# A fused layer on one core: other steps for the sums and row copies of its attention, and 52 norm tiles on ScalarE

## Chip, core and metric

One core of a Trainium2 chip runs the whole program as one launch. The metric is the device time of one execution, in microseconds (us); lower is better. The core has five engines that take their instructions in order and wait for each other by counting semaphores: TensorE (PE), VectorE (DVE), ScalarE (ACT), GpSimd (POOL) and SyncE, which issues the DMAs.

## The reference

The input is 16 batches of 256 tokens of 128 numbers, float32. Four sublayers follow each other, each added to its input: a long convolution, a mixture of 8 experts (top 2), an attention, the same experts again. Each reads a layer norm of the stream. The change is in the attention:

```python
x = x + _L0_attn_b_ref(_layernorm(x, axis=-1), W_attn, W_proj)
# _L0_attn_b_ref: 16 heads of 8, four sets of queries, one set of keys and values
qkv = x @ W_attn.T
for g in range(4):
    att = softmax(where(causal, q_g @ k.T / sqrt(8), -inf))
    outs.append(att @ v)
return concatenate(outs, -1) @ W_proj.T
```

## The kernel before

**Stages.** Convolution, first experts, attention and second experts follow each other. While the attention runs, the last chunks of the first experts' result are normed for it, and its own results are normed for the second experts. A chunk is 4 tiles of 128 tokens, two batches.

**Time of the attention.** It runs in 256 steps, 16 in each batch: 4 quads of 4 heads, and 4 steps t = 0 to 3 in each quad. A step makes scores of heads against keys on TensorE (`tensor_scores`, line 1269) into one half of six PSUM banks, 1280 columns. Steps take the two halves in turn, so the scores of step n wait until the exp of step n-2 has read that half. ScalarE makes the exp of all 1280 columns in one instruction (`scalar_exp`, line 1296) into one of 8 buffers `prob`. GpSimd sets the masked entries to zero with affine selects, six in each quad (`gpsimd_mask`, line 1328).

**Blocks of tokens.** The 256 tokens of a batch are cut into four blocks of 64. The input holds the second half of the tokens in reverse. Blocks of queries against blocks of keys make three kinds of work: EARLY, ACROSS and LATE. EARLY and ACROSS have 512 columns a head (four query sets, two blocks), LATE 256. A quad's four steps hold each kind for each of its four heads (`STEPS_Q`, line 60).

**Sums.** `tensor_weigh` (line 1348) multiplies the values with the probabilities of one kind, 4 heads beside each other, as 8 instructions, adding ACROSS, EARLY and LATE up in bank 7. It is called for the quad before in steps 1, 2 and 3: `SUMS_Q = (ACROSS, EARLY, LATE)`. ACROSS waits until VectorE has turned the previous quad's sums out of bank 7. EARLY and LATE wait for masks. Value rows lie in `vstack`.

**VectorE's part.** `vector_turn` (line 1370) reads the finished sums with a stream transpose, inverts the denominators and scales, three instructions; `vector_rows` (line 1386) turns a batch's result for the projection, three transposes. `vector_attended` (line 1436) adds the projection to the stream. `vector_at_x_high` and `_low` copy the transposed tokens of batch b+2 out of PSUM in two float16 parts, `vector_qk_high` and `_low` the same for queries and keys, `vector_v` copies value rows. `vector_bounds` (line 1398) tests the inverted denominators once in four batches. Layer norms: statistics on VectorE (line 369), the power on GpSimd (line 383), and the tiles, (x - mean) * rstd, on VectorE (line 388), 4 in a chunk, two at step 9 and two at step 13.

**What is beside what.** No planner: the order of each engine is written out by step. In each step TensorE issues scores, then what `tensor_beside` (line 1834) holds for it, then the sum:

```python
if b + 2 < BATCH and at == 0:            tensor_at_x(e, b + 2)
if b + 2 < BATCH and at in (4, 8, 12):   tensor_qk(e, b + 2, at // 4 - 1)
if 0 < b < BATCH - 1 and at in (7, 11):  tensor_project(e, b - 1, at // 8)
if b + 1 < BATCH and at == 15:           tensor_v(e, b + 1)
```

Token transposes (line 1124), q/k products (1168), projections (1432) and value rows (1235) all use bank 6, so each waits until VectorE has copied the one before out of it: transposes wait for `v_copied`, q/k products of steps 8 and 12 for `attn_done` (the projection of the batch before is added), projections for `lo_done` and for `rows_up`. VectorE's order beside is in `vector_beside` (line 1871): rows at step 5, residuals at 6 and 10, value copies at 14, the turn ahead of all else at step 3 of a quad. In the first 16 steps nothing is projected. SyncE writes and reads back q/k parts through DRAM for the batches ahead; the change leaves that as it is.

After the last step, `tensor_second` (line 1722) sums the last quad between the first products of the second experts.

Of the kernel before, what the change touches and what calls it, by code (L numbers as in the profile page):

```python
# [13 lines left out]
ALU = mybir.AluOpType  # L14
# [3 lines left out]
P = 128  # L18
# [46 lines left out]
SUMS_Q = (ACROSS, EARLY, LATE)  # L65
STEPS_B = 4 * QUADS
SUMS_B = len(SUMS_Q) * QUADS
# [77 lines left out]
def build_in(nc, dr, out, ctx):  # L145
# [150 lines left out]
    def new_norm(tag):  # L296
# [21 lines left out]
        "conv_mean_negated", "offset_ready", "mean_negated", "route_offset", "conv_normed_by_scalar", "first_folded", "fold_sums", "fold_differences"))  # L318

# [445 lines left out]

    def tensor_xt(e, m, ch):
# [345 lines left out]
    def tensor_at_x(e, b):  # L1112
# [10 lines left out]
        for at, h in ((0, 1), (P, 1), (P + BLK, 0)):  # L1123
            last = e.transpose(bank(at_bank(b))[:, at:at + P], normed[:, HALVES * b + h, :], eye[:])
        last.then_inc(at_up, 1)
# [3 lines left out]

# [92 lines left out]
    def tensor_v(e, b):  # L1222
# [7 lines left out]
        for kind in (EARLY, LATE, ACROSS):  # L1230
            for i, (w_part, x_part) in enumerate(PRODUCTS):
                for half in range(HALVES if kind != ACROSS else 1):
                    rows = slice(BLK * half, BLK * (half + 1)) if kind != ACROSS else slice(0, P)
                    token = P * half + BLK * kind if kind != ACROSS else P
# [34 lines left out]
    def tensor_scores(e, n):  # L1269
# [12 lines left out]
        for kind, lane, col in STEPS_Q[t]:  # L1282
            at = slice(SLOT * lane, SLOT * (lane + 1))
            queries = qstack[at, s, c].rearrange("p g (h l q) -> p h l g q", h=HALVES, q=BLK)
            for half in range(HALVES):
                rows = slice(BLK * half, BLK * (half + 1))
                if kind == EARLY:
                    key, moving, place = P * half, queries[:, half], to[rows, col:col + BANK]
                elif kind == LATE:
                    key, moving, place = P * half + BLK, queries[:, half, 1], to[rows, col:col + SETS * BLK]  # L1290
                else:
                    key, moving, place = P + BLK * half, queries[:, 0], to[rows, col:col + BANK]
# [3 lines left out]
    def scalar_exp(e, n):  # L1296
        if n >= PROBS:
            e.wait_ge(weighed, len(SUMS_Q) * ((n - PROBS) // 4 + 1))
# [29 lines left out]
    def gpsimd_mask(e, n):  # L1328
# [3 lines left out]
        if t == 0:  # L1332
            gpsimd_second_half_mask(e, m)
            if q:
                gpsimd_first_half_mask(e, m - 1)
# [4 lines left out]
        elif t == 3:  # L1340
            gpsimd_second_half_mask(e, m + 2)

# [27 lines left out]
    def vector_turn(e, t):  # L1370
        b, c, _ = step_of(4 * t)
        r = t % 2
        e.wait_ge(weighed, len(SUMS_Q) * (t + 1))
# [12 lines left out]
    def vector_rows(e, b):  # L1386
        e.wait_ge(o_normed, QUADS * (b + 1))
        if b:
            e.wait_ge(projected, HALVES * b)

        blocks = o_norm[:, 0].rearrange("p (g l n) r -> p g l (n r)", g=SETS, l=2)
        rows = o_rows[:, 0].rearrange("p g (l t) -> p g l t", l=2)
        for late in range(2):
            e.transpose(rows[:, :, 1 - late], blocks[:, :, late])  # L1394
        e.transpose(o_rows[:, 1].rearrange("p g t -> p (g t)"), o_norm[:, 1].rearrange("p n r -> p (n r)"))\
         .then_inc(rows_up, 1)
# [19 lines left out]
    def tensor_project(e, b, h):  # L1416
        e.wait_ge(rows_up, b + 1)
# [822 lines left out]
```

## Time and profile before

| what | value |
|---|---|
| three runs | 790.78, 791.18, 791.28 us; median 791.18 |
| the profiled execution | 789.12 us, its span 787.4 us |
| busy share of the span | PE 93%, ACT 86%, DVE 84%, POOL 71% |
| attention, first exp to last | starts at 245.1 and 592.8 us of the span |
| granted TensorE clock | 0.999 of full speed over the span |

Busy time is a union of instruction durations; ends of matmuls are modelled, so distances between starts are the firmer reading. "idle ... <- X" is the time an engine stood still just before instructions and what released it. PE is the multiplying part of TensorE, PEld its weight loads. Line numbers are those of the kernel before.

### The profile page before, as it was taken

Reading aid. Unit: us, or ns where it says so; the run is one execution under the profiler, and the core shown is the slowest. Engines: PE = TensorE matmul, PEld = TensorE weight load, DVE = VectorE, ACT = ScalarE, POOL = GpSimd, SP = SyncE. Lnnn points to the kernel's source line nnn. Section 1 sums busy time; section 2 is a strip of 40 time slices with the busy share of each in tenths; the row PEclk is TensorE's granted clock in tenths of the full one; section 3 lists DMA queues with packets and bytes.
Section 4 is the critical chain, followed back from the end, with each engine's and each line's share of the span. In section 5 each row is a group of like instructions: output and inputs, shape, how many; then the busy total and the mean of one; then the engine's idle time right before and its main releaser. Section 6 shows DMA issues by size and latency. Waiting matters only on the chain.

```text
span 787.4 us, 21234 instructions
## 1 busy us (share of the span) xinstructions
PE 736.1 (93%) x8090; PEld 404.9 (51%) x8090; DVE 660.6 (84%) x1955; ACT 677.5 (86%) x934; POOL 562.6 (71%) x623
## 2 busy tenths in 40 slices
PE   5798999999999999999999999999888999999996
PEld 3345667777775233333333333333334777677774
DVE  7998999899876867879788888788487889989885
ACT  5918999999999988888898898888987999899984
POOL 2898676655446989999999999989995445445542
PEclk9999999999999999999999999999999999999999
DMA  9210000000044244533543333453400000000000
GB/s 271 64 80 28 2 2 2 2 2 2 2 109 109 73 95 97 101 87 89 108 108 100 96 97 98 92 96 82 99 2 1 10 7 14 15 15 15 15 14 18
DMA packets 37964, 45.74 MB, mean 58 GB/s; under 512 B 6137, under 2 KB 23810, under 8 KB 37858
## 3 DMA queue, kind: packets, MB, share of 16 engines
q1 hardware_dynamic: 37858, 44.33, 23.0%
q8 instruction: 66, 1.08, 0.6%
q14 instruction: 40, 0.33, 0.2%
HBM read 27.53 MB, written 16.78 MB: 56 GB/s over the span
## 4 chain that ended last, share of the span: by engine, by line
PE 61%; DVE 24%; issue 6%; ACT 5%; POOL 4%; DMA 0%; DVEq 0%; ACTq 0%; POOLq 0%
PE psum L1015 15%; PE psum L1365 14%; PE psum L946 14%; PE psum L1432 4%; PE psum L1293 4%; DVE mixed L1034 4%; PE psum L1168 3%; DVE o_tok L1375 2%; DVE vstack L1261 2%; PE psum L1235 2%; ACT hidden_first L960 1%; ACT hidden_parts_first L962 1%; PE psum L695 1%; DVE parts L1193 1%; DVE o_rows L1394 1%
## 5 line engine op out<-in xcount | busy, mean ns | idle before, releaser
L1300 ACT ACTIVATE prob<-psum 128x1280 f32<-128x1280 f32 x256 | 304.6, 1240 | 43.0 <-PE psum L1293 36.3
L1309 POOL TENSOR_SCALAR_AFFINE_SELECT prob<-prob 128x768 f32<-128x768 f32 (+1 forms) x384 | 308.1, 840 | 27.0 <-ACT prob L1300 26.9
L946 PE MATMUL psum<-xt_parts,w_parts 128*128 128x512 f16 x768 | 186.6, 379 | 0.0
L1365 PE MATMUL psum<-prob,vstack 128*32 128x512 f32 (+1 forms) x1536 | 177.3, 533 | 6.4 <-DVE o_tok L1375 4.4
L976 POOL TENSOR_TENSOR hidden_parts_second<-hidden_second,hidden_parts_second 128x512 f16<-128x512 f32 x64 | 77.7, 1213 | 94.8 <-ACT hidden_parts_second L962 94.8
L1034 DVE SCALAR_TENSOR_TENSOR mixed<-psum,comb_y,mixed 128x128 f32<-128x128 f32 x512 | 143.1, 339 | 1.6 <-PE psum L1015 1.5
L976 POOL TENSOR_TENSOR hidden_parts_first<-hidden_first,hidden_parts_first 128x512 f16<-128x512 f32 x64 | 79.2, 1238 | 73.0 <-ACT hidden_parts_first L962 73.0
L1293 PE MATMUL psum<-qstack,kstack 32*64 32x512 f16 (+1 forms) x1536 | 103.4, 362 | 1.9 <-ACT prob L1300 1.8
L1293 PEld LDWEIGHTS psum<-qstack,kstack 32*64 32x64 f16 x1536 | 29.9, 101 | 145.9 <-ACT prob L1300 125.2
L946 PEld LDWEIGHTS psum<-xt_parts,w_parts 128*128 128x128 f16 x768 | 70.9, 98 | 64.9 <-issue 1.4
L960 ACT ACTIVATE hidden_second<-psum,b 128x512 f32<-128x512 f32 x128 | 88.3, 690 | 17.3 <-PE psum L946 12.3
L1015 PEld LDWEIGHTS psum<-w_parts,hidden_parts_first 128*128 128x128 f16 x1536 | 90.3, 98 | 19.6 <-issue 6.7
L1015 PE MATMUL psum<-w_parts,hidden_parts_first 128*128 128x128 f16 x1536 | 96.2, 219 | 3.9 <-DVE mixed L1034 3.4
L1015 PEld LDWEIGHTS psum<-w_parts,hidden_parts_second 128*128 128x128 f16 x1536 | 90.8, 98 | 16.5 <-issue 2.5
L1015 PE MATMUL psum<-w_parts,hidden_parts_second 128*128 128x128 f16 x1536 | 96.0, 219 | 1.0 <-POOL hidden_parts_second L976 0.5
L960 ACT ACTIVATE hidden_first<-psum,b 128x512 f32<-128x512 f32 x128 | 90.3, 705 | 7.2 <-PE psum L946 6.4
L962 ACT ACTIVATE hidden_parts_first<-psum,b 128x512 f16<-128x512 f32 x128 | 90.5, 707 | 0.0
L962 ACT ACTIVATE hidden_parts_second<-psum,b 128x512 f16<-128x512 f32 x128 | 88.4, 691 | 0.0
L969 DVE TENSOR_TENSOR hidden_parts_second<-hidden_second,hidden_parts_second 128x512 f16<-128x512 f32 x64 | 57.3, 896 | 17.8 <-ACT hidden_parts_second L962 17.8
L1375 DVE STREAM_TRANSPOSE o_tok<-psum 128x512 f32<-128x512 f32 x64 | 45.7, 713 | 25.4 <-PE psum L1365 25.4
L969 DVE TENSOR_TENSOR hidden_parts_first<-hidden_first,hidden_parts_first 128x512 f16<-128x512 f32 x64 | 49.6, 776 | 16.9 <-ACT hidden_parts_first L962 16.9
L1365 PEld LDWEIGHTS psum<-prob,vstack 128*32 128x32 f32 x1536 | 30.2, 108 | 45.4 <-issue 28.0
(150 smaller groups left out, 859.6 us busy)
## 6 DMA issues: line engine op xcount, KB each, us to landing
qstack<-qk_parts SPq DMA_DIRECT2D x128, 128.0 KB, 3.6
qk_parts<-parts SPq DMA_DIRECT2D x64, 192.0 KB, 3.2
kstack<-qk_parts SPq DMA_DIRECT2D x128, 32.0 KB, 3.5
stream<-u_folded SPq DMA_DIRECT2D x4, 512.0 KB, 8.2
kept_x<-stream SPq DMA_DIRECT2D x4, 512.0 KB, 2.7
out<-mixed SPq DMA_DIRECT2D x7, 256.0 KB, 2.3
w_whole<-L_ffn_W SPq DMA_DIRECT2D x1, 1024.0 KB, 9.6
taps<-c_taps SPq DMA_DIRECT2D x1, 640.0 KB, 7.7
```

The source lines that it names most:

```text
L946: last = e.matmul(bank(u % 4), m.w1[:, w_part, ex, cols], xt_parts[:, s, x_part, :], start=(n == 0), stop=(n == len(PRODUCTS) - 1))
L960: last = e.activation(m.hidden[:, r, k, :], bank(u % 4), ACT.Relu, scale=scale, bias=bias)
L962: last = e.activation(m.hidden_parts[:, r, 0, k, :], bank(u % 4), ACT.Relu, scale=scale, bias=bias)
L969: e.tensor_tensor(m.hidden_parts[:, r, 1, 0, :], m.hidden[:, r, 0, :], m.hidden_parts[:, r, 0, 0, :], ALU.subtract).then_inc(low_first, 1)
L976: e.tensor_tensor(m.hidden_parts[:, r, 1, 1, :], m.hidden[:, r, 1, :], m.hidden_parts[:, r, 0, 1, :], ALU.subtract).then_inc(low_second, 1)
L1015: last = e.matmul(down_place(m, ch, ex, t), h_[:, t * P:(t + 1) * P], w_, start=(n == 0), stop=(n == len(terms) - 1))
L1034: last = e.scalar_tensor_tensor(out=m.y[:, t0 + t, :], in0=down_place(m, ch, ex, t), scalar=comb_y[:, s, t, ex:ex + 1], in1=m.y[:, t0 + t, ...
L1293: last = e.matmul(place, kstack[at, s, c, key:key + BLK], moving, start=True, stop=True)
L1300: e.activation(prob[:, n % PROBS, 0:COLS], psum[:, TILE * (n % 2):TILE * (n % 2) + COLS], ACT.Exp, scale=SCALE)\
L1309: return e.affine_select(kept, kept, [[0, n] for n in kept.shape[1:-1]] + [[sign, BLK]], ALU.is_ge, 0.0, base=BLK * half, channel_multipli ...
L1365: last = e.matmul(to[SLOT * lane:SLOT * (lane + 1)], vstack[:, b % 2, kind, c * LANES + lane].rearrange("p h r -> p (h r)"), weights_of(q, ...
L1375: e.transpose(o_tok[:, r, :].rearrange("p (g l t) -> p g l t", l=2, t=BLK), by_token).then_inc(turned, 1)
```

## The change

- EARLY and LATE sums of the quad before stand together in step 2, ACROSS alone in step 1, nothing in step 3 (`SUMS_Q`). The turn moves from step 3 to step 2.
- Blocks get other kinds, so that EARLY and LATE use 128 rows of one token stretch: 12 products for value rows in place of 15. The three token transposes write the blocks to other places.
- Token transposes move from step 0 to step 2, their copies on VectorE too, ahead of the turn. Rows move from step 5 to 3, residuals from 6 and 10 to 7 and 11, value copies from 14 to 15. Rows are released in two parts, each to its projection.
- The second mask of a LATE pair moves to step 3, from the next quad's step 0.
- 13 chunks' norm tiles move to ScalarE: x * rstd + offset with Identity, behind the exps of steps 9 and 13; VectorE makes offset = -mean * rstd for 4 tiles in one instruction at step 6.

```diff
@@ -62,9 +62,11 @@
 COLS = 2 * BANK + SETS * BLK
-SUMS_Q = (ACROSS, EARLY, LATE)
+SUMS_Q = ((), (ACROSS,), (EARLY, LATE), ())
+KINDS = 3
 STEPS_B = 4 * QUADS
-SUMS_B = len(SUMS_Q) * QUADS
+SUMS_B = KINDS * QUADS
 MASKS_Q = 3
@@ -316,6 +318,7 @@
         "conv_mean_negated", "offset_ready", "mean_negated", "route_offset", "conv_normed_by_scalar", "first_folded", "fold_sums", "fold_differences"))
+    beside_offset = sem("offset_beside_attention")
@@ -762,6 +765,50 @@
+    @dataclass
+    class Beside:
+        norm: object
+        i: int
+        x: object
+        ch: int
+        n: int
+    def chunk_normed(b):
+        if b % 2 == 0 and b // 2 + 2 < FFN_CHUNKS:
+            return mixed_norm, b // 2 + 2
+        return (expert_norm, (b - 3) // 2) if b % 2 and b >= 3 else None
+    def normed_beside(b):
+        held = chunk_normed(b)
+        if held is None:
+            return None
+        norm, ch = held
+        n = sum(chunk_normed(before) is not None for before in range(b))
+        return Beside(norm, ch, mixed, ch, n) if norm is mixed_norm else Beside(norm, second.at + ch, stream, ch, n)
+    def vector_offset_beside(e, of):
+        tiles = slice(of.ch * FFN_TILES, (of.ch + 1) * FFN_TILES)
+        e.wait_ge(of.norm.rstd, of.i + 1)
+        e.scalar_tensor_tensor(out=offset[:, tiles], in0=meanvar[:, tiles, 0], scalar=-1.0, in1=rstd[:, tiles],
+                               op0=ALU.mult, op1=ALU.mult).then_inc(beside_offset, 1)
+    def scalar_normed_beside(e, of, half):
+        if half == 0:
+            e.wait_ge(beside_offset, of.n + 1)
+            if of.norm is mixed_norm:
+                e.wait_ge(xt_up, of.ch + 1)
+            else:
+                e.wait_ge(at_up, FFN_TILES // HALVES * (of.ch + 1))
+        t0 = of.ch * FFN_TILES + half * FFN_TILES // 2
+        for t in range(t0, t0 + FFN_TILES // 2):
+            last = e.activation(normed[:, t, :], of.x[:, t, :], ACT.Identity, scale=rstd[:, t:t + 1],
+                                bias=offset[:, t:t + 1])
+        if half:
+            last.then_inc(of.norm.out, 1)
@@ -1120,13 +1167,14 @@
-        for at, h in ((0, 1), (P, 1), (P + BLK, 0)):
-            last = e.transpose(bank(at_bank(b))[:, at:at + P], normed[:, HALVES * b + h, :], eye[:])
-        last.then_inc(at_up, 1)
+        to = bank(at_bank(b))
+        for at in (0, P + BLK):
+            e.transpose(to[:, at:at + P], normed[:, HALVES * b + 1, :], eye[:])
+        e.transpose(to[:, P:3 * P].rearrange("p (l h t) -> p l h t", h=HALVES, t=BLK)[:, :, 0], normed[:, HALVES * b, :],
+                    eye[:]).then_inc(at_up, 1)
@@ -1229,9 +1277,9 @@
             for i, (w_part, x_part) in enumerate(PRODUCTS):
-                for half in range(HALVES if kind != ACROSS else 1):
-                    rows = slice(BLK * half, BLK * (half + 1)) if kind != ACROSS else slice(0, P)
-                    token = P * half + BLK * kind if kind != ACROSS else P
+                for late in range(2 if kind == ACROSS else 1):
+                    rows = slice(BLK * late, BLK * (late + 1)) if kind == ACROSS else slice(0, P)
+                    token = P * late + BLK if kind == ACROSS else P * kind
                     last = e.matmul(bank(6)[rows, kind * P:(kind + 1) * P],
@@ -1281,21 +1329,21 @@
             at = slice(SLOT * lane, SLOT * (lane + 1))
-            queries = qstack[at, s, c].rearrange("p g (h l q) -> p h l g q", h=HALVES, q=BLK)
+            queries = qstack[at, s, c].rearrange("p g (l h q) -> p h l g q", h=HALVES, q=BLK)
             for half in range(HALVES):
...
                 if kind == EARLY:
-                    key, moving, place = P * half, queries[:, half], to[rows, col:col + BANK]
+                    key, moving, place = BLK * half, queries[:, half], to[rows, col:col + BANK]
                 elif kind == LATE:
-                    key, moving, place = P * half + BLK, queries[:, half, 1], to[rows, col:col + SETS * BLK]
+                    key, moving, place = P + BLK * half, queries[:, half, 1], to[rows, col:col + SETS * BLK]
                 else:
-                    key, moving, place = P + BLK * half, queries[:, 0], to[rows, col:col + BANK]
+                    key, moving, place = P * half + BLK, queries[:, 0], to[rows, col:col + BANK]
                 last = e.matmul(place, kstack[at, s, c, key:key + BLK], moving, start=True, stop=True)
...
         if n >= PROBS:
-            e.wait_ge(weighed, len(SUMS_Q) * ((n - PROBS) // 4 + 1))
+            e.wait_ge(weighed, KINDS * ((n - PROBS) // 4 + 1))
         e.wait_ge(scored, n + 1)
@@ -1331,14 +1379,13 @@
             gpsimd_second_half_mask(e, m)
-            if q:
-                gpsimd_first_half_mask(e, m - 1)
         elif t == 1:
...
             gpsimd_second_half_mask(e, m + 2)
+            gpsimd_first_half_mask(e, m + 2)
@@ -1370,7 +1417,7 @@
         r = t % 2
-        e.wait_ge(weighed, len(SUMS_Q) * (t + 1))
+        e.wait_ge(weighed, KINDS * (t + 1))
         by_token = bank(7).rearrange("p (l g t) -> p g l t", l=2, t=BLK)
@@ -1387,13 +1434,14 @@
             e.wait_ge(projected, HALVES * b)
+        e.transpose(o_rows[:, 1].rearrange("p g t -> p (g t)"), o_norm[:, 1].rearrange("p n r -> p (n r)"))\
+         .then_inc(rows_up, 1)
...
         for late in range(2):
-            e.transpose(rows[:, :, 1 - late], blocks[:, :, late])
-        e.transpose(o_rows[:, 1].rearrange("p g t -> p (g t)"), o_norm[:, 1].rearrange("p n r -> p (n r)"))\
-         .then_inc(rows_up, 1)
+            last = e.transpose(rows[:, :, 1 - late], blocks[:, :, late])
+        last.then_inc(rows_up, 1)
@@ -1414,7 +1462,7 @@
     def tensor_project(e, b, h):
-        e.wait_ge(rows_up, b + 1)
+        e.wait_ge(rows_up, HALVES * b + h + 1)
         if b + 3 < BATCH:
@@ -1832,7 +1880,7 @@
     def tensor_beside(e, b, at):
-        if b + 2 < BATCH and at == 0:
+        if b + 2 < BATCH and at == 2:
             tensor_at_x(e, b + 2)
@@ -1854,8 +1902,9 @@
             tensor_beside(e, *STARTS[n])
-            if n >= 4 and n % 4:
-                tensor_weigh(e, n // 4 - 1, SUMS_Q[n % 4 - 1])
+            if n >= 4:
+                for kind in SUMS_Q[n % 4]:
+                    tensor_weigh(e, n // 4 - 1, kind)
@@ -1863,38 +1912,36 @@
             scalar_exp(e, n)
+            b, at = STARTS[n]
+            if at in (9, 13) and normed_beside(b):
+                scalar_normed_beside(e, normed_beside(b), at // 12)
             if n == LAST - STEPS_B:
...
     def vector_beside(e, b, at):
-        if b + 2 < BATCH and at == 0:
-            vector_at_x_high(e, b + 2)
-            vector_at_x_low(e, b + 2)
         if b + 2 < BATCH and at in (4, 8, 12):
...
             vector_qk_low(e, b + 2, at // 4 - 1)
-        if b and at == 5:
+        if b and at == 3:
             vector_rows(e, b - 1)
...
             vector_bounds(e, b // BOUNDED - 1, at // 4)
-        if b and at in (6 if b + 1 < BATCH else 9, 10):
-            vector_attended(e, b - 1, at // 10)
-        if b + 1 < BATCH and at == 14:
+        if b and at in (7 if b + 1 < BATCH else 9, 11):
+            vector_attended(e, b - 1, at // 11)
+        if b + 1 < BATCH and at == 15:
...
                 vector_mixed_stats(e, b // 2 + 2)
-            elif at in (9, 13):
-                vector_mixed_normed_half(e, b // 2 + 2, at // 12)
         if b % 2 and b >= 3:
...
                 vector_route_stats(e, second, (b - 3) // 2)
-            elif at in (9, 13):
-                vector_second_normed_half(e, (b - 3) // 2, at // 12)
+        if at == 6 and normed_beside(b):
+            vector_offset_beside(e, normed_beside(b))
         if b == 12 and at % 2:
@@ -1909,9 +1956,13 @@
         for n in range(LAST):
-            if n % 4 == 3 and n >= 4:
+            b, at = STARTS[n]
+            if at == 2 and b + 2 < BATCH:
+                vector_at_x_high(e, b + 2)
+                vector_at_x_low(e, b + 2)
+            if n % 4 == 2 and n >= 4:
                 vector_turn(e, n // 4 - 1)
-            vector_beside(e, *STARTS[n])
+            vector_beside(e, b, at)
@@ -1923,7 +1974,6 @@
             gpsimd_mask(e, n)
-        gpsimd_first_half_mask(e, MASKS_Q * QUADS * BATCH - 1)
```

## Rows read from the trace of the kernel before

**Rows 1.** page, section 4: the chain that ended last, by engine

```profile
PE 61%; DVE 24%; issue 6%; ACT 5%; POOL 4%; DMA 0%; DVEq 0%; ACTq 0%; POOLq 0%
```

**Rows 2.** page, section 5: the exps and the masks

```profile
L1300 ACT ACTIVATE prob<-psum 128x1280 f32<-128x1280 f32 x256 | 304.6, 1240 | 43.0 <-PE psum L1293 36.3
L1309 POOL TENSOR_SCALAR_AFFINE_SELECT prob<-prob 128x768 f32<-128x768 f32 (+1 forms) x384 | 308.1, 840 | 27.0 <-ACT prob L1300 26.9
```

**Rows 3.** batch 6: us, then busy us of PE, PEld, DVE, ACT, POOL, clock, DMA

```profile
375.77:397.49 21.72, 21.10 (x241) 7.77 (x241) 17.45 (x42) 19.09 (x16) 19.96 (x26) 1.00 0.45 98
```

**Rows 4.** timeline of batch 6, PE: start us, us, engine, line, op, names, count

```profile
376.87 1.07 PE L1365 MATMUL psum<-prob,vstack 128*32 128x512 f32 x8
377.87 0.41 PE L1293 MATMUL psum<-qstack,kstack 32*64 32x512 f16 x6
...
379.54 0.64 PE L1365 MATMUL psum<-prob,vstack 128*32 128x256 f32 x8
380.11 0.41 PE L1293 MATMUL psum<-qstack,kstack 32*64 32x512 f16 x6
380.45 0.83 PE L1168 MATMUL psum<-at_x,wqkv_parts 128*128 128x256 f16 x6
381.21 0.41 PE L1293 MATMUL psum<-qstack,kstack 32*64 32x512 f16 x6
...
383.87 0.41 PE L1293 MATMUL psum<-qstack,kstack 32*64 32x512 f16 x6
384.46 1.16 PE L1432 MATMUL psum<-wproj,o_rows 128*128 128x128 f32 x8 [0.18 <-DVE o_rows L1395]
385.55 0.64 PE L1365 MATMUL psum<-prob,vstack 128*32 128x256 f32 x8
...
395.66 0.80 PE L1235 MATMUL psum<-wqkv_parts,at_x 128*64 128x128 f16 x15
396.39 0.64 PE L1365 MATMUL psum<-prob,vstack 128*32 128x256 f32 x8
396.96 0.41 PE L1293 MATMUL psum<-qstack,kstack 32*64 32x512 f16 x6
397.80 0.52 PE L1124 MATMUL psum<-eye,normed 128*128 128x128 f32 x3 [0.44 <-DVE vstack L1261]
```

**Rows 5.** timeline of batch 6, ACT: the first exp of batch 7

```profile
397.49 1.24 ACT L1300 ACTIVATE prob<-psum 128x1280 f32<-128x1280 f32 x1 [0.40 <-PE psum L1293]
```

**Rows 6.** timeline of batch 0, where PE waited for an exp

```profile
248.78 3.50 ACT L1300 ACTIVATE prob<-psum 128x1280 f32<-128x1280 f32 x3 [0.61 <-PE psum L1293]
...
250.07 0.41 PE L1293 MATMUL psum<-qstack,kstack 32*64 32x512 f16 x6 [0.60 <-ACT prob L1300]
```

**Rows 7.** waits between 270 and 620 us: in total, times, longest

```profile
PE psum L1124 <- DVE vstack L1261: 5.3, 12, 0.4
PE psum L1432 <- DVE o_rows L1395: 5.0, 13, 1.3
```

**Rows 8.** timeline of batch 6, DVE: a turn, the next copy, a residual

```profile
380.24 0.72 DVE L1375 STREAM_TRANSPOSE o_tok<-psum 128x512 f32<-128x512 f32 x1 [0.57 <-PE psum L1365]
...
381.73 0.68 DVE L1193 TENSOR_SCALAR parts<-psum 128x512 f16<-128x512 f32 x1
...
385.65 0.29 DVE L1442 TENSOR_TENSOR stream<-psum,mixed 128x128 f32<-128x128 f32 x1 [1.25 <-PE psum L1432]
```

**Rows 9.** groups by line, 270 to 620 us: the upper bound test

```profile
L1407 DVE SCALAR_TENSOR_TENSOR in_bounds<-rden,in_bounds 128x512 f32<-128x512 f32 x3 | 3.2, 1065 | 0.0
```

**Rows 10.** timeline of the first expert layer, ACT: four norm tiles

```profile
64.00 1.67 ACT L747 ACTIVATE normed<-stream,offset,rstd 128x128 f32<-128x128 f32 x4
65.53 0.70 ACT L960 ACTIVATE hidden_first<-psum,b 128x512 f32<-128x512 f32 x1
```

**Rows 11.** timeline at the end of the attention, PE

```profile
592.14 0.41 PE L1293 MATMUL psum<-qstack,kstack 32*64 32x512 f16 x6
...
595.62 1.06 PE L1365 MATMUL psum<-prob,vstack 128*32 128x512 f32 x8 [2.50 <-DVE o_tok L1375]
```

## The prediction

> **What bounds the kernel now.** I read the chain of waits first. TensorE holds 61% of the chain that ended last, VectorE 24% and ScalarE 5% [rows 1]. The change touches the attention, the stretch of 256 exps; there ScalarE sat idle 43.0 us before exps, 36.3 of them for score products on TensorE [rows 2]. So I asked for one batch of the attention by itself, batch 6 counted from 0: 21.72 us long, with TensorE busy 21.10 us, GpSimd 19.96, ScalarE 19.09 and VectorE 17.45 [rows 3]. The reader should see that TensorE has no room, and ScalarE 2.63 us.
>
> TensorE's timeline of that batch gives the price of each piece, taken from its start to the start of the next one, for the ends are modelled [rows 4]. One step's scores take 0.335 us (0.34 from 380.11 to 380.45, 0.33 in others), a sum over ACROSS or EARLY 1.00 (376.87 to 377.87), over LATE 0.57 (379.54 to 380.11), a q/k product 0.76, a projection half 1.09, the value rows 0.73. Two places are longer than that: from the scores at 383.87 to the projection 0.59, hence 0.255 of waiting for rows, and from the scores at 396.96 to the token transposes 0.84, hence 0.505 of waiting for VectorE's value copies. Work is then 21.72 - 0.255 - 0.505 = 20.96 us.
>
> Two more distances decide this case. An exp begins 0.53 to 0.54 us after its scores begin, when ScalarE is idle (396.96 [rows 4] to 397.49 [rows 5]), and lasts 1.24. Scores begin 0.05 us after the exp that frees their half of PSUM: the exp that began at 248.78 ended at 250.02, and TensorE, idle 0.60 us, began at 250.07 [rows 6]. PSUM holds two steps. So from the start of step n's scores to the start of step n+2's scores there lie **at least 0.54 + 1.24 + 0.05 = 1.83 us**, whatever TensorE has to do.
>
> **Why the old order rarely meets that floor.** The sums lie at steps 1, 2 and 3 of each quad, ACROSS, EARLY, LATE. Around the light steps 3 and 0, step 3's LATE and whatever lies beside fill the time: 0.335 + 0.57 + 0.335 + 0.76 = 2.00, more than 1.83. In rows 6 there are no sums yet at steps 2 and 3, and there TensorE waits; that is the case the new order makes everywhere.
>
> **The change, part by part.**
>
> *Sums.* EARLY and LATE both come at step 2, none at step 3. The number of products stays. Step 2 becomes 1.57 us of sums after its scores, so step 3's scores come late, ScalarE idles before its exp, and that exp begins 0.54 us after them. Then the floor of 1.83 runs from step 3.
> - Step 15 to step 1 of the next batch: TensorE has 0.335 + value rows + 0.335. The value rows go from 15 products to 12, EARLY and LATE on 128 rows at once: 0.73 x 12/15 = 0.58. That is 1.25 of work against 1.83: a **wait of 0.58**, where the token transposes (moved to step 2) used to stand.
> - Step 3 to step 5: 0.335 + 0.335 + 0.76 = 1.43 against 1.83: **0.40**.
> - Steps 7 and 11 carry a projection, 1.09, so the floor is met there: nothing.
>
> *Residual behind the projection.* The q/k product of step 8 waits until VectorE has read the projection of step 7 out of the same bank. LATE used to stand between the two; now only the scores of step 8 do. Count from the end of LATE at step 6. TensorE: 0.335 + 1.09 + 0.335 = 1.76. VectorE: it starts the turn 0.13 us after LATE's slot ended (380.11 [rows 4], 380.24 [rows 8]), and is free again 1.49 us later (381.73); then comes the new offset operation, 4 columns, about 0.25 by my estimate from such short ones, bounds 0.15 and 0.6; then the residual, 0.29 and some 0.07 to the release. Together 0.13 + 1.49 + 0.25 + 0.36 = 2.23, a **wait of 0.47**, or 0.22 in batches without a norm. Step 12 has no offset: **0.22**. In batches 5, 9 and 13 the upper bound test, 1.07 us [rows 9], stands in that same chain at step 6 and adds its length.
>
> *Waits taken away.* The token transposes at step 2 no longer stand behind the value copies, and the rows are turned at step 3, long before step 7. The two waits were 5.3 and 5.0 us over 12 and 13 batches in the stretch from 270 to 620 us [rows 7]. By start distances I count 0.505 and 0.255.
>
> *Norms.* 52 tiles leave VectorE, 4 in each of 13 batches; ScalarE makes them, behind the exps of steps 9 and 13. ScalarE had four in a row from 64.00 to the next instruction at 65.53, 0.385 each [rows 10]: 0.77 at each place, 1.54 in a batch, 20.0 in all. It had 2.63 us idle [rows 3]. The norms push the exp of steps 10 and 14 back by up to 0.77, but the exp behind it waits for the scores of steps 11 and 15, which stand behind the double sum and come about that much late themselves. So I take **0**, with only 0.1 us to spare; uncovered they cost up to 20.0. VectorE is not the bound, so its relief is also worth 0, except at the end.
>
> *Sum for batch 6.* Work 20.96 - 0.15 = 20.81; waits 0.58 + 0.40 + 0.47 + 0.22 = 1.67; 22.48 against 21.72: +0.76.
>
> *Sum for the stage.* New waits: 14 x 0.58 = 8.1; 13 x 0.40 = 5.2 (batch 0 has it already); 11 x 0.47 + 2 x 0.22 + 3 x 1.07 = 8.8; 13 x 0.22 = 2.9; together 25.0. Gone: 14 x 0.505 = 7.1; the waits for rows 5.0, with 13 x 0.08 for start distances 6.0; value rows 15 x 0.15 = 2.3; together 15.4. Net +9.6.
>
> *The end.* After the last scores at 592.14 TensorE's next sum came at 595.62, with 2.50 us idle for VectorE, whose turn stood behind two norm tiles [rows 11]. Now that turn comes one step earlier and the tiles are gone; the sum needs only the last exp, 1.83 + 0.02 after the scores: 3.48 - 1.85 = -1.6 us. Against it, in batch 15 the first transposes still wait for value copies, and with no LATE in between for 0.57 more; I add 0.6 for that and 0.5 for masks and startup, where GpSimd is closest to its limit. Total **+9.1**. The profiled execution took 789.1, which gives 798.2; the median of the runs is 791.2, 2.1 above it, so I forecast **800.3**.
>
> **A rule against this reading.** TensorE's 21.10 of 21.72 us is my reason to call it the bound; its timeline shows distances that repeat to 0.01 us. The Trainium skill (Perfetto Trace Analysis, Identifying the Most-Contended Engine) says that matmul busy time does not show how near TensorE is to its limit, and that occupancy does for the others. By it GpSimd or ScalarE would be asked first, and what ScalarE is given would count in full: the second rival below.
>
> **Rivals.**
> 1. *TensorE waits for nothing.* If scores don't meet the floor, because the pairs of sums run closer together than two separate ones and ScalarE catches up, only the removed waits count: 15.4 + 1.6 = 17.0 less, 774; with half of the new waits 787. It decides from where the new waits sum to less than 15.9 instead of 25.0. For it: TensorE is the bound and its waits fall. Against it: rows 6 show the wait where no sum stands, and the floor holds two rows' distances only. Chance 0.12. If LATE right behind EARLY saves 0.1 us, 64 times, that is 794, still in my forecast.
> 2. *ScalarE becomes the bound.* If an activation from SBUF between two exps costs more than 0.385, or the exp behind it can't overlap it, the 0.1 us to spare is gone at 26 places: 20.0 more at the very most, about 820; with a quarter of it 805. Against: 2.63 us idle. Chance 0.08.
> 3. *Nothing to speak of.* The two orders give each other back what they take: the pieces are the same, and GpSimd, 19.96 of 21.72, sets the pace after all, as 384 masks of 0.84 [rows 2] don't change. Then 789.6 to 792.8. Against: the last mask of a quad is ready about 1.3 us before LATE needs it, by two short masks behind the exp of step 3 against 0.05 + 0.335 + 1.00 + 0.335 + 1.00. Chance 0.06.
>
> **The numbers.** Forecast 0.74, its own range 793 to 807. Under 788 lies most of rival 1, over 807 a part of rival 2; so 788 to 807. A measurement of this kernel tells 0.2%, 1.6 us. Faster 0.13, same 0.06, slower 0.81.
>
> **What would show it.** In a middle batch: length 22.4 to 22.5; TensorE idle for ScalarE before the scores of steps 1 and 5, 0.6 and 0.4; before the q/k products of steps 8 and 12 for VectorE, 0.5 and 0.2, and over 1 at step 8 in batches 5 and 9; ScalarE idle about 0.6 or more before each exp of a step 3; no wait before the transposes and projections; about 1.5 us between last exp and the next work less than before. A middle batch under 21.7 or ScalarE without idle time would prove me wrong.

## The result, and the profile after

The changed kernel took 814.34 us (median of 4 runs, 813.36 to 819.12), against 791.23 for the kernel before beside it: ratio 1.0304, 95% interval 1.0263 to 1.0345. It is 23.1 us slower. The forecast had the side right (slower, 0.81) and the size wrong: 800.3, range 788 to 807.

The page of the kernel after, sections 1, 2 (the clock alone) and 5 (the exps, as in [rows 2]):

```profile
span 812.2 us, 21151 instructions
...
PE 735.3 (91%) x8042; PEld 411.7 (51%) x8042; DVE 638.8 (79%) x1916; ACT 692.8 (85%) x986; POOL 565.3 (70%) x623
...
PEclk9999999999999999998999999999999999999999
...
L1348 ACT ACTIVATE prob<-psum 128x1280 f32<-128x1280 f32 x256 | 302.4, 1241 | 52.8 <-PE psum L1341 52.4
```

Every engine's share fell, TensorE's busy time is what it was (735.3 us against 736.1), and the span grew by 24.8 us. So time was lost in waits, of all engines at once. The attention, from the first exp to the end of the last, grew from 348.9 to 374.9 us (it ran from 245.1 to 620.0); what follows it shrank by 1.1.

TensorE's waits, 270 to 620 us, as in [rows 7] (in total, times, longest):

```profile
PE psum L1216 <- DVE stream L1490: 22.7, 26, 2.5
...
PE psum L1341 <- ACT prob L1348: 14.9, 30, 1.3
```

Both old waits, for value copies and for rows, are gone, as foreseen; only the first transposes of the second experts, in batch 15, still wait for value copies, 1.9 us. L1216, the q/k product, waits 22.7 us for the residual L1490, L1341, the scores, 14.9 us for exps. Batch 6 of the kernel after, TensorE, from the first scores behind the exps of steps 15 and 3 to the product of step 8, as in [rows 4]:

```profile
385.63 0.41 PE L1341 MATMUL psum<-qstack,kstack 32*64 32x512 f16 x6
385.97 0.80 PE L1283 MATMUL psum<-wqkv_parts,at_x 128*128 128x128 f16 x12
386.70 0.41 PE L1341 MATMUL psum<-qstack,kstack 32*64 32x512 f16 x6
387.46 0.41 PE L1341 MATMUL psum<-qstack,kstack 32*64 32x512 f16 x6 [0.35 <-ACT prob L1348]
...
391.04 0.52 PE L1341 MATMUL psum<-qstack,kstack 32*64 32x512 f16 x12
391.50 0.83 PE L1216 MATMUL psum<-at_x,wqkv_parts 128*128 128x256 f16 x6
392.87 0.41 PE L1341 MATMUL psum<-qstack,kstack 32*64 32x512 f16 x6 [0.54 <-ACT prob L1348]
...
394.54 1.50 PE L1412 MATMUL psum<-prob,vstack 128*32 128x512 f32 x16
395.97 0.41 PE L1341 MATMUL psum<-qstack,kstack 32*64 32x512 f16 x6
396.30 1.16 PE L1480 MATMUL psum<-wproj,o_rows 128*128 128x128 f32 x8
397.39 0.41 PE L1341 MATMUL psum<-qstack,kstack 32*64 32x512 f16 x6
399.26 0.81 PE L1216 MATMUL psum<-at_x,wqkv_parts 128*128 128x256 f16 x6 [1.46 <-DVE stream L1490]
```

Two readings. From the scores of step 15 at 385.63 to those of step 1 at 387.46 lie 1.83 us, and from step 3 at 391.04 to step 5 at 392.87 again 1.83: the floor of the forecast, to the hundredth. But the product of step 8 waited 1.46, not 0.47. What VectorE did meanwhile, as in [rows 8]:

```profile
396.10 0.72 DVE L1422 STREAM_TRANSPOSE o_tok<-psum 128x512 f32<-128x512 f32 x1 [0.60 <-PE psum L1412]
396.86 0.35 DVE L1425 RECIPROCAL rden<-o_tok 128x32 f32<-128x32 f32 x1
397.25 1.15 DVE L1427 TENSOR_TENSOR o_norm<-o_tok,rden 128x256 f32<-128x256 f32 x1
398.31 0.60 DVE L796 SCALAR_TENSOR_TENSOR offset<-meanvar,rstd 128x4 f32<-128x4 f32 x1
398.84 0.28 DVE L1490 TENSOR_TENSOR stream<-psum,mixed 128x128 f32<-128x128 f32 x1
```

The order is the one forecast; the scaling of the turn took 1.15 us where the turn's 1.49 [rows 8] has it at 0.42, and four columns of offset took 0.60. In that time GpSimd's masks ran without a pause:

```profile
395.50 5.00 POOL L1357 TENSOR_SCALAR_AFFINE_SELECT prob<-prob 128x768 f32<-128x768 f32 x6
```

The clock is the second thing. Stretches of the kernel after (us, busy us of PE, PEld, DVE, ACT, POOL, granted clock, DMA share, GB/s); [rows 3] has 1.00 for batch 6 of the kernel before:

```profile
369.00:381.00 12.00, 9.48 (x81) 3.67 (x74) 6.42 (x11) 6.62 (x8) 7.67 (x9) 0.72 0.32 65
387.30:410.40 23.10, 20.47 (x238) 8.12 (x238) 16.30 (x40) 20.27 (x22) 20.29 (x25) 1.00 0.37 93
410.30:435.00 24.70, 22.06 (x238) 8.24 (x238) 16.30 (x40) 20.41 (x22) 20.29 (x25) 0.93 0.36 86
```

In batch 5 (first line) the bound test stands in the chain too, the product of step 8 waited 2.52 us, and with that wait TensorE's granted clock fell from 2.4 to 1.2 GHz for 6.8 us:

```profile
373.62 1.44 PE L1216 MATMUL psum<-at_x,wqkv_parts 128*128 128x256 f16 x6 [2.52 <-DVE stream L1490]
374.99 0.64 PE L1341 MATMUL psum<-qstack,kstack 32*64 32x512 f16 x6
375.56 1.94 PE L1412 MATMUL psum<-prob,vstack 128*32 128x512 f32 x8
377.42 0.64 PE L1341 MATMUL psum<-qstack,kstack 32*64 32x512 f16 x6
```

A q/k product took 1.37 us from start to start instead of 0.76, an ACROSS sum 1.86 instead of 1.00. The same happened in batches 0, 7, 9 and 15 for 3.4 us each. That has its price in the lengths: a middle batch took 23.05 us, but batch 7, with the same waits, 24.64, batch 5 26.70 and batch 9 25.62.

### The profile page after: what moved, and what is told of

Its sections match the earlier page's. It is cut to its first block and busy times, and to the rows that moved or that the text cites. A ratio compares the mean times of both kernels' runs of the same rounds, so it can differ in the third digit from the quotient of the medians.

```text
span 812.2 us, 21151 instructions
## 1 busy us (share of the span) xinstructions
PE 735.3 (91%) x8042; PEld 411.7 (51%) x8042; DVE 638.8 (79%) x1916; ACT 692.8 (85%) x986; POOL 565.3 (70%) x623
## 3 DMA queue, kind: packets, MB, share of 16 engines
q8 instruction: 66, 1.08, 0.6%
## 5 line engine op out<-in xcount | busy, mean ns | idle before, releaser
L1412 PE MATMUL psum<-prob,vstack 128*32 128x512 f32 (+1 forms) x1536 | 170.2, 546 | 1.9 <-ACT prob L1348 1.9
L1341 PE MATMUL psum<-qstack,kstack 32*64 32x512 f16 (+1 forms) x1536 | 101.5, 368 | 17.6 <-ACT prob L1348 17.6
L1007 ACT ACTIVATE hidden_second<-psum,b 128x512 f32<-128x512 f32 x128 | 88.3, 690 | 15.9 <-PE psum L993 12.3
L1341 PEld LDWEIGHTS psum<-qstack,kstack 32*64 32x64 f16 x1536 | 28.9, 102 | 122.7 <-ACT prob L1348 84.5
L1412 PEld LDWEIGHTS psum<-prob,vstack 128*32 128x32 f32 x1536 | 37.2, 110 | 71.0 <-issue 64.9
```

The source lines that it names most:

```text
L1007: last = e.activation(m.hidden[:, r, k, :], bank(u % 4), ACT.Relu, scale=scale, bias=bias)
L1341: last = e.matmul(place, kstack[at, s, c, key:key + BLK], moving, start=True, stop=True)
L1412: last = e.matmul(to[SLOT * lane:SLOT * (lane + 1)], vstack[:, b % 2, kind, c * LANES + lane].rearrange("p h r -> p (h r)"), weights_of(q, ...
```

## Experiments

Medians of the kernel before beside them were 790.7 to 790.9 us. A middle batch is one like batch 6.

### Norms back on VectorE, norms alone on ScalarE

```diff
 # norms_on_vector, against the changed kernel: 52 tiles by
-                scalar_normed_beside(e, normed_beside(b), at // 12)
-            vector_offset_beside(e, normed_beside(b))
+                vector_mixed_normed_half(e, b // 2 + 2, at // 12)
+                vector_second_normed_half(e, (b - 3) // 2, at // 12)
 # scalar_norms_old_order, against the kernel before: the same the other way round
```

> The changed kernel with its 52 norm tiles back on VectorE (mean and rstd, at steps 9 and 13), the offset operation gone. Theory 1 (TensorE waits behind VectorE's chain turn, offset, residual at step 8, and behind the exps of steps 3 and 15): only the offset's 0.6 us leaves that chain, so a middle batch falls from 23.05 to about 22.4 us, some of the half-clock stretches go, and the time is 800 to 809. Theory 2 (the norms on ScalarE are what costs): all of the loss goes, 789 to 795.

> The kernel before with the 52 norm tiles alone moved to ScalarE (scale and offset, behind the exps of steps 9 and 13), all sums, rows, transposes and residuals at their old steps. Theory 1: ScalarE's idle time covers them, and the residual stands ahead of the offset operation: 788 to 795, a middle batch 21.7 to 22.0. Theory 2: most of the loss shows here too, 805 to 815.

With the norms back: 801.98 us, ratio 1.0166 (1.0130 to 1.0202); a middle batch 22.52. With the norms alone moved: 789.67 us, ratio 0.9993 (0.9982 to 1.0004); middle batches 21.72, as before, with the waits of [rows 7] unchanged (5.3 and 4.9 us). Theory 1 holds in both, theory 2 in neither. In the new order, too, ScalarE's tiles don't hold TensorE: with them back on VectorE it still waited 0.35 and 0.54 us for exps in a middle batch, as in the changed kernel. ScalarE's 52 tiles cost nothing in the old order (28 and 24 of them):

```profile
L804 ACT ACTIVATE normed<-stream,offset,rstd 128x128 f32<-128x128 f32 x28 | 12.2, 490 | 0.0
L804 ACT ACTIVATE normed<-mixed,offset,rstd 128x128 f32<-128x128 f32 x24 | 10.5, 493 | 0.0
```

In the new order what costs is the offset on VectorE, 0.53 us in a middle batch (23.05 - 22.52; the wait at step 8 fell from 1.46 to 0.94), about 6 us over 11 batches with a projection and a norm; the rest of those 12.4 us are clock stretches that are gone (in this run two of 3.4 us stand in the attention, where there were 20.4 us).

### The q/k product one step later

```diff
-        if b + 2 < BATCH and at in (4, 8, 12):
+        if b + 2 < BATCH and at in (4, 9, 13):
```

> The changed kernel with the q/k products of steps 8 and 12 (and VectorE's copies of them) at steps 9 and 13, so that TensorE has scores and more between a projection and the product that waits for its residual. Theory 1: the wait of 1.46 and 0.22 us in a batch goes, nearly all of it, the floor behind the exps stays: a middle batch 21.4 to 22.2 us, no half-clock stretch, 788 to 799. If the waits behind the exps were the larger part instead, the batch stays above 22.5 and the time above 803.

A miss: 807.85 us, ratio 1.0233 (1.0209 to 1.0258), a middle batch 22.69. By the bound in the expectation the larger part would go to the waits for exps. The trace says why it doesn't: in a middle batch the product still waited 1.05 us for the residual. Step 8 has no sum in the new order, so going from step 8 to step 9 passes only one set of scores, 0.335 us. The expectation had counted a step as a step of the old order. The next run takes the wait away by another edit.

### The residual ahead of the turn

```diff
 # on VectorE, batches 1 to 14: at steps 6 and 10 no turn;
 # at steps 7 and 11, after vector_beside has issued the residual:
+            if behind:
+                vector_turn(e, n // 4 - 1)
```

> The changed kernel with one thing different on VectorE: in batches 1 to 14 the turn that belongs to steps 6 and 10 comes behind the residual of steps 7 and 11, so that the residual no longer stands behind the turn, only behind the offset operation. Theory 1 (the chain turn, offset, residual holds the q/k product of step 8): the wait of 1.46 us falls to 0.1 to 0.3, that of 0.22 to about 0.1, a middle batch is 21.4 to 21.9 us, the half-clock stretches behind those waits go, and the time is 788 to 796. If the chain is not what holds it, or the turn is then late for the next ACROSS sum, the batch stays over 22.5 and the time over 803.

793.49 us, ratio 1.0034 (1.0019 to 1.0049): of 23 us lost, 20 are back with one reordering on VectorE. A middle batch is 21.72, the q/k products wait 0.27 us in it, and the scores still 0.97 for exps. TensorE and clock in the same two stretches as above:

```profile
369.00:381.00 12.00, 11.43 (x140) 4.21 (x139) 8.27 (x19) 11.63 (x14) 10.91 (x15) 1.00 0.44 96
387.30:410.40 23.10, 21.85 (x258) 8.69 (x251) 15.96 (x40) 21.28 (x22) 21.78 (x28) 1.00 0.38 93
```

After batch 0 the clock no longer fell in the attention of this profiled execution (791.27 us, mean clock 0.992). That isn't so of every execution: seven of the ten had a mean clock of 0.986 to 0.988 and took 793.3 to 794.9 us, so some stretches stay; where they lie, no trace shows. What remains of the loss is less than batch 0 alone, 25.36 us instead of 20.81, in which the products of step 4 waited 1.25 us for the token copies and the clock fell for 6.8 us.

### Small masks

```diff
-            return prob[:, slot].rearrange("p (n l g q) -> p n l g q", n=3, l=2, q=BLK)[:, :, 0]
-        return prob[:, slot:slot + 2, 2 * BANK:COLS].rearrange("p n (g q) -> p n g q", q=BLK)
+            return prob[:, slot].rearrange("p (n l g q) -> p n l g q", n=3, l=2, q=BLK)[:, 0:1, 0]
+        return prob[:, slot:slot + 1, 2 * BANK:COLS].rearrange("p n (g q) -> p n g q", q=BLK)
```

> The changed kernel with each mask cut to a third or a half of its columns (256 in place of 768 and 512), so most masked entries stay in the sums: a part of the masking is left out. Theory 1a (VectorE's operations with two SBUF inputs wait for a mask in progress on GpSimd, which makes the scaling of the turn 1.15 us long at step 6 and the offset 0.6): the scaling at step 6 falls towards 0.42 to 0.6, the offset towards 0.1 to 0.3, the wait before the q/k product of step 8 from 1.46 to 0.4 to 0.8, a middle batch to 22.0 to 22.4. Theory 1b (the scaling is long for another reason): nothing changes there.

This kernel leaves out most of the masking. 792.79 us (one execution), a middle batch 21.87, a little under its range; TensorE waited 0.50 us for residuals in it instead of 1.68. Of the 1.18 us that the batch lost, 1.17 are the wait at step 8 (0.29 for 1.46), while the waits for exps stayed 0.35 and 0.54. VectorE's two operations, 280 to 580 us, first with small masks, then in the changed kernel:

```profile
L1427 DVE TENSOR_TENSOR o_norm<-o_tok,rden 128x256 f32<-128x256 f32 x54 | 22.9, 425 | 1.9
L796 DVE SCALAR_TENSOR_TENSOR offset<-meanvar,rstd 128x4 f32<-128x4 f32 x11 | 2.3, 211 | 0.0
```

```profile
L1427 DVE TENSOR_TENSOR o_norm<-o_tok,rden 128x256 f32<-128x256 f32 x51 | 29.8, 585 | 1.8
L796 DVE SCALAR_TENSOR_TENSOR offset<-meanvar,rstd 128x4 f32<-128x4 f32 x11 | 6.6, 602 | 0.0
```

Scaling 425 ns against 585, offset 211 against 602: theory 1a. Nothing in those operations changed, only how long GpSimd's instructions beside them are. The trace of the changed kernel says it of each operation. Of the 63 scalings in the attention 44 took 0.50 us or less; the other 19 took 0.78 to 1.16, and each of them ended 0.27 us after a mask did. The 11 offsets of 0.60 us all ended within 0.01 us after a mask; the two that met no mask in progress took 0.15.

The Trainium skill (SBUF — State Buffer, SBUF: two separate sides) says that a VectorE operation with two SBUF inputs and a GpSimd operation that reads SBUF contend for a shared port pair, and that whichever starts first holds it for its whole instruction. The trace agrees for the masks: the scaling, two SBUF inputs, took 1.15 us beside long ones and 0.425 on average beside short ones, and its late ends follow theirs. It isn't seen with every GpSimd instruction: the scaling in the turn of [rows 8], 0.42 us at 381.38, ran beside GpSimd's power of 4 columns, recorded from 381.33 for 1.00 us (spans on GpSimd are rough). The forecast had no term for any of this.

### The sums alone

```diff
-SUMS_Q = (ACROSS, EARLY, LATE)
+SUMS_Q = ((), (ACROSS,), (EARLY, LATE), ())
 # turn at n % 4 == 2, second LATE mask at step 3; nothing else of the change
```

> The kernel before with the sums and what goes with them alone moved: EARLY and LATE at step 2, the turn at step 2, the second mask of a LATE pair at step 3; the old blocks, norms on VectorE, transposes at step 0, rows at 5, residuals at 6 and 10, value copies at 14 stay. Theory 1: this alone brings most of the loss: waits behind the exps of step 3 (0.4 to 0.55) and, at step 0, for value copies with nothing beside them (0.5 becomes about 1.1), and the residual behind the turn, 0.5 to 1.2 at step 8; a middle batch 22.5 to 23.6, the time 803 to 820. Theory 3 (the loss needs the moved transposes and residuals too): 790 to 799.

827.17 us, ratio 1.0462 (1.0440 to 1.0485), above the range that I gave: the sums alone cost 36 us, so the rest of the change gives 13 back. Where they cost (270 to 620 us):

```profile
PE psum L1125 <- DVE vstack L1262: 17.6, 12, 1.5
PE psum L1169 <- DVE stream L1442: 13.2, 26, 1.9
PE psum L1294 <- ACT prob L1301: 9.5, 16, 1.1
```

The token transposes at step 0 wait 1.47 us for value copies each time, 17.6 us in all, where it was 5.3 before [rows 7]; in the changed kernel, with the transposes at step 2, this wait is gone. Batches without a bound test took 23.02 us at full clock and 24.7 to 24.8 with a half-clock stretch; ten such stretches stand in the attention after batch 0.

### LATE back at step 3

```diff
-SUMS_Q = ((), (ACROSS,), (EARLY, LATE), ())
+SUMS_Q = ((), (ACROSS,), (EARLY,), (LATE,))
 # turn at step 3, rows at 5, residuals at 6 and 10, value copies at 14;
 # the second run, in batch 0 alone: transposes and copies at step 0
-        if b + 2 < BATCH and at == 2:
+        if b + 2 < BATCH and at == (2 if b else 0):
```

> The changed kernel with LATE sums back at step 3, the turn with them, residuals at 6 and 10, rows at 5, value copies at 14; the new blocks, the norms on ScalarE, the transposes at step 2 and the rows in two parts stay. Theory 1: both kinds of waits go, since LATE stands again between scores of steps 3 and 0 and between projection and q/k product: TensorE without waits, a middle batch 20.9 to 21.6, 780 to 790. Theory 2: ScalarE's norms stay, so 805 to 815.

> The kernel with LATE back at step 3, and in batch 0 alone the token transposes and their copies at step 0 as in the kernel before, ahead of the statistics on VectorE. In the run without this TensorE waited 1.25 us at step 4 of batch 0 and the clock then stood at half for 3.4 us. Theory 1: that wait and that stretch go, batch 0 falls from 23.6 to 21.0 to 22.3 us, the time to 785 to 787.5. If the clock falls all the same, 787.5 to 789.

788.05 us, ratio 0.9969 (0.9954 to 0.9985), and with the repair of batch 0 786.05 us, ratio 0.9945 (0.9928 to 0.9962): both beat the changed kernel by over 26 us, the second one the kernel before by 4.7. Batch 0 fell from 23.61 to 20.83 us, 2.78 less: its wait of 1.25 and, so, 1.53 for a stretch of 3.4 us at half clock (its range was 21.0 to 22.3). No wait for residuals is left in a middle batch; its length, 21.70, missed its range of 20.9 to 21.6 by 0.1, since one wait for an exp is left (batch 7 of the second run):

```profile
394.33 0.41 PE L1341 MATMUL psum<-qstack,kstack 32*64 32x512 f16 x6
394.67 0.80 PE L1283 MATMUL psum<-wqkv_parts,at_x 128*128 128x128 f16 x12
395.40 0.64 PE L1412 MATMUL psum<-prob,vstack 128*32 128x256 f32 x8
395.96 0.41 PE L1341 MATMUL psum<-qstack,kstack 32*64 32x512 f16 x6
396.85 0.41 PE L1341 MATMUL psum<-qstack,kstack 32*64 32x512 f16 x6 [0.48 <-ACT prob L1348]
```

Steps 15 and 0 hold 0.34 + 0.73 + 0.56 + 0.34 = 1.97 us, more than the floor, yet the scores of step 1 wait. Here the exp of step 15 began 1.23 us after its scores, since the two norm tiles behind the exp of step 13 had pushed the exps of steps 14 and 15. Taking the old wait of 0.505 away had opened another of 0.48. So a middle batch is as long as before (21.70 against 21.72); the gain over the kernel before stands in batches whose waits were longer than in a middle one (batches 1 and 12, 0.8 and 0.9 us shorter) and behind the attention (191.9 us against 193.3). Three more runs asked whether the wait can be closed.

### What still holds the middle batch

```diff
 # norms_at_7_and_11, against the last kernel
-            if at in (9, 13) and normed_beside(b):
+            if at in (7, 11) and normed_beside(b):
-        if at == 6 and normed_beside(b):
+        if at == 5 and normed_beside(b):
 # turn_ahead_of_values: that, and value copies at step 15, behind the turn
-        if b + 1 < BATCH and at == 14:
+        if b + 1 < BATCH and at == 15:
```

> The kernel with LATE back at step 3 and the repaired batch 0, with ScalarE's norm tiles behind the exps of steps 7 and 11 in place of 9 and 13, and the offset at step 5. In the run without this ScalarE sat idle 0.76 and 0.38 us before the exps of steps 8 and 12, and none before that of step 15, whose lateness (0.48 us before the scores of step 1) I put down to the norms of step 13. If so: that wait goes, a middle batch is 21.1 to 21.4, the time 779 to 783. If the wait of 0.48 has another source, the batch stays at 21.7 and the time at 785 to 787.

> The same kernel with LATE at step 3 and the repaired batch 0, with the norm tiles back on VectorE at steps 9 and 13. If the norms on ScalarE cause the 0.48 us: a middle batch 21.2 to 21.5, the time 780 to 785, with some loss at the end of the attention, where the last turn stands behind two norm tiles again (about 1.5 us). If they don't: 785 to 789.

> The kernel with LATE at step 3, the repaired batch 0 and ScalarE's norms at steps 7 and 11, with one thing more: VectorE's value copies at step 15, behind the turn in place of ahead of it. In the run without this the ACROSS sum of step 1 waited 0.79 us for that turn, which stood behind 1.16 us of value copies. If that is the last hold of the middle batch: the wait falls to 0.2 to 0.4, the token transposes of step 2 may wait up to 0.4 for the value copies, a middle batch is 21.0 to 21.5, the time 777 to 784. If a third constraint keeps 21.70, the time stays at 785 to 787.

All three missed their favoured ranges, and the last two lay above both of theirs. Norms at 7 and 11: 786.09 us, ratio 0.9944 (0.9931 to 0.9956), the middle batch still 21.70. The cause of the 0.48 was right, no exp is waited for there any more; but the turn behind the value copies took its place at once:

```profile
397.56 1.06 PE L1412 MATMUL psum<-prob,vstack 128*32 128x512 f32 x8 [0.79 <-DVE o_tok L1422]
```

Norms on VectorE with LATE at step 3: 790.97 us, ratio 1.0006 (0.9995 to 1.0018), middle batches 21.96, with 0.88 us of that same wait. In this order ScalarE's norms are thus worth 5 us (790.97 against 786.05). The turn ahead of the value copies: 797.1 us, ratio 1.0085 (1.0072 to 1.0099). The wait for the turn fell to 0.31 as expected, but the value copies came so late that the transposes waited 1.03:

```profile
400.87 0.85 DVE L1427 TENSOR_TENSOR o_norm<-o_tok,rden 128x256 f32<-128x256 f32 x1
401.64 1.15 DVE L1309 TENSOR_SCALAR vstack<-psum 64x256 f32<-64x256 f32 x3
...
404.25 0.41 DVE L1186 CAST at_x<-psum 128x256 f16<-128x256 f32 x1
```

The scaling took 0.85 us where a mask ran beside it. So between the sums of step 15 and those of step 2 VectorE has a turn and the value copies, about 2.7 us, and whichever comes second is waited for. 786.05 us is the best that these runs reached.

## Why the prediction was right or wrong

**Right: what bounds, the floor, the waits that go.** TensorE's time is work plus waits; the distance of 1.83 us came out to the hundredth, at both places; both old waits went. ScalarE's norms cost TensorE nothing in the old order and in the new one, as two runs show: 22.7 us more work for ScalarE, and 789.67 us; rival 2 falls, and so does the reading by occupancy that stood behind it. The end of the attention gained 1.2 us against 1.6 (from the last scores to the next sum 2.26 us instead of 3.48).

**Sizes in the middle batch, forecast and measured:**

| term, by start distances | forecast | measured |
|---|---|---|
| scores of step 1, for the exp of 15 | 0.58 | 0.43 |
| scores of step 5, for the exp of 3 | 0.40 | 0.61 |
| q/k product of step 8, for the residual | 0.47 | 1.54 |
| q/k product of step 12 | 0.22 | 0.29 |
| a double sum, four in a batch | 1.57 | 1.43 |
| value rows, 12 products | 0.58 | 0.73 |
| scores of steps 3 and 4 together | 0.67 | 0.46 |
| batch | 22.48 | 23.05 |

The two floor terms together are 0.98 against 1.04. The step that failed is the third: "0.13 + 1.49 + 0.25 + 0.36 = 2.23, a **wait of 0.47**". It took the turn's length from one place [rows 8] as if it were fixed, and the offset from short operations. Both depend on what GpSimd does at that moment. The rest of the chain was right: with small masks the term came to 0.37, and the forecast's own chain gives 0.38 with the 0.16 that the offset took there in place of 0.25. The trace of the kernel before already held the price, ten scalings of 0.66 to 0.95 us in its attention. Its turn at 386.25 met only the last 0.23 us of a mask; its scaling took 0.50 us, and the next masks began after it:

```profile
387.39 0.50 DVE L1380 TENSOR_TENSOR o_norm<-o_tok,rden 128x256 f32<-128x256 f32 x1
```

```profile
387.96 4.71 POOL L1309 TENSOR_SCALAR_AFFINE_SELECT prob<-prob 128x768 f32<-128x768 f32 x6 [0.33 <-ACT prob L1300]
```

In the new order the turn before step 8 falls into a row of six masks. Scaling 0.73 more (1.15 for 0.42) and offset 0.35 more (0.60 for 0.25) make 1.08, and the term came out 1.07 larger; over 11 batches that is 11.8 us. The value rows failed too: I scaled 0.73 by 12/15, but 12 products took as long as 15. The traces say why. Products of 64 rows start in pairs, less than 0.01 us apart, and from one pair to the next it is mostly 0.05 to 0.06 us, as between two products of 128 rows. The kernel before had 6 pairs and 3 products of 128 rows, the changed one has 3 pairs and 6 products: 9 places in both.

**Wrong by omission: the clock and batch 0.** No term of the sum held the possibility that the clock falls behind longer waits. In the profiled execution six drops, five of them in the attention, came to 20.4 us at half speed there. Batches 5, 7 and 9 were 2.6, 1.6 and 1.5 us longer than waits explain (26.70 - 23.05 - 1.06; 24.64 - 23.05; 25.62 - 23.05 - 1.05), batch 0 by 1.5, as its repair shows, and batch 15 by my estimate some 1.5 too, from products stretched in the same way: about 9 us. Batch 0 also holds a wait that the forecast put at nothing: its token copies, moved to step 2, came 1.25 us late for the q/k product of step 4.

**The whole difference.** The forecast of the profiled execution was 798.2 us, and it took 814.3: 16.1. Chain +11.8, clock +9, value rows 15 x 0.15 = +2.3, floors and step 12 some +1.5, double sums 64 x 0.14 = -9.0, pairs of scores 14 x 0.21 = -2.9, batch 0 +1.25, the first transposes of batch 15 some +1.0 (they waited 1.93 us for value copies), the end +0.4; together +15.4, so 0.7 stay open. Between the medians the difference is only 14.0: the forecast added the 2.1 us by which the profiled execution of the kernel before lay under its median, and that of the changed kernel lay at its median. That the double sums gave 9.0 us back, which the forecast had named only as a possible 0.1 us each, is luck for the total.

**The signs.** TensorE's waits came where they were named. ScalarE's idle time of 0.6 before each exp of a step 3 did not: in batch 6 it was 0.78 at step 3, 0.30 at step 7 and none at steps 11 and 15, where the norm tiles had filled it.

**Rival 1** fell: new waits of 37.6 us (22.7 and 14.9), more than the 25.0 of the forecast and not less than 15.9. Its premise came true in part, pairs of sums did run closer together. **Rival 3** fell with it, but its engine mattered in a way that I had not asked: GpSimd set no pace, it stretched VectorE's chain.

## What to carry to other kernels

Work between a producer and the step that reuses its buffer is cover: when sums are gathered into one step, the light steps left over uncover every chain that they hid, on all engines. Before moving an operation, look at what runs beside its new place on the engine that shares its port, and price it from rows where that neighbour is busy, not from the row of its old place. And a wait that grows to a microsecond or two can be charged twice on TensorE, once itself and once as half clock behind it.

## What had not been expected of the hardware

- The scaling of 128x256 with two SBUF inputs took 0.42 us in many places, 1.15 or 0.85 beside a running mask, and the long ones ended 0.27 us after a mask did; four columns of offset took 0.60 beside masks, 0.21 on average with masks of 256 columns.
- The granted clock fell to half in stretches of 3.4 or 6.8 us after waits of 1.25 us (batch 0) and 2.5 us (batch 5), and also in batch 7, whose waits were those of batch 6, where it didn't. With the wait of 1.46 gone it stayed up in all batches from 1 on in the profiled execution. Why one of two equal batches loses its clock stays open.
- Two sums one behind the other took 1.43 us from start to start instead of 1.00 + 0.57, 0.14 less.
- Two products of 64 rows that start as a pair took no longer, from start to start, than one of 128 rows.
